# Attention stage of a fused kernel: the second chunk's projections laid over other units, later chunks turned two units later

## The chip, the cores and the metric

One core of one Trainium2 chip runs the whole program in one launch. The metric is the device time of one execution in microseconds (us), lower is better. The kernel before was timed three times.

## The reference

The input is x[8, 256, 128] in float32 (2048 tokens of 128 numbers). Four parts follow one another, each on the layernorm of x and added back to x: four Mamba layers, a feed-forward block with 4-bit block quantisation of inputs, weights and hidden values, an attention block, and the same feed-forward block again. The change touches the attention block alone, which computes:

```
qkv = layernorm(x) @ w_qkv.T + b_qkv            # 16 heads of 8 numbers
att = (q k^T) / sqrt(8) + bias[h, i - j]        # HoPE bias per head
att = softmax(where(j <= i, att, -inf))         # 256 x 256 per head
x   = x + (att v) @ w_proj.T + b_proj
```

## The kernel before, in words

The tokens lie in 16 tiles of 128, and in four chunks (0 to 3) of four tiles, which is two batches. Attention works through 64 **units** u; a unit is two heads of one batch (`where`, L1663), so 16 units make a chunk. The loop of every engine runs over the same list, `ITERATIONS` = -3 to 69 (L1476), and asks `iteration(u)` (L1525) what is to be done. A unit below 0 belongs to the lead.

In iteration u the pieces are, in order: `s` (the scores of unit u+3, for the row maxima alone), `t0` and `t1` (the turned scores of unit u), for odd u `peak` (the maxima of two units turned) and `mix` (probabilities times v, two units at a time, three units late), for even u `turn` (that result turned back), and every eight units `ctx` and `proj` (the output projection, of which `ctx` comes at u = 12, 20, 28, ... and `proj` one unit later). A chunk's inputs are made in four more pieces: `x` turns the normed rows with four TensorE transposes (`turn_x`, L1689), `q` and `k` are one projection each (`project`, L1696), `v` is four matmuls (`project_v`, L1702). Chunk 0 is made before the loop. Chunk 1 is made in the lead, one piece each in units -3 (x), -2 (q), -1 (k) and 0 (v). Chunks 2 and 3 are made at u % 16 = 2 (x), 6 (q), 8 (k) and 9 (v), so chunk 2 in units 2, 6, 8, 9 and chunk 3 in units 18, 22, 24, 25 (`EARLY` is 2).

Each piece needs a PSUM bank, and `Banks` (L1479) counts the uses in the order in which `iteration` names them: `s` alternates between two double banks s0 and s1; `t0` and `t1` have one each; `peak`, `turn`, `proj` and `v` share one bank, here called bank v; `mix`, `x`, `q`, `k` and `ctx` share another, bank a. A piece on TensorE waits until the use before it of its bank has been read.

Who reads what. On TensorE `both_scores` (L1735) starts each iteration with the two mask matmuls of the `s` bank (`mask_scores`, L1710); the turned scores wait until the maxima of their pair were added into q (`banks.wait_read(t, "peak", u // 2)`) and until the exponentials of the unit before left banks t0 and t1. On VectorE iteration u does, in this order: `add_row` of a peak (L1851), `norm.vector_normalise` of a chunk if u % 16 is 2 (L1057), the maxima of `s` (L1843, L1844), the reading of `turn`, `proj` and `v` (`values`, L1835), and `norm.vector_moments` if u % 16 is 0 (L1038, L1042). ScalarE does `exps` (two exponentials, L1958), then `norm.scalar_rstd` if u % 16 is 1, then the copies of `mix`, `x`, `q`, `k` and `ctx`: `copy_mixed` (L1965), `copy_x` (L1944, it also waits for the v projection of the chunk before, which reads the same xT), `add_bias` (L1950), `copy_context` (L1971). GpSimd masks the probabilities (`causal`, L1915) and adds the output bias (L1920). SyncE waits for each `add_bias` and then issues four DMAs (L1685) that lay q or k of the chunk into the strips of `att_qk`; the scores of chunk 1 read them first in iteration 13 (`s` of unit 16), and `add_bias` of chunk 2 waits for those of chunk 1.

Of the kernel before, what the change touches and what calls it, by code (L numbers as in the profile page):

```python
# [1474 lines left out]
MAX_ROW = 2 * HD  # L1475
S_LEAD, PV_LAG, TURN_LAG, OUT_LAG = 3, 3, 4, 12  # L1476
EARLY = 2
ITERATIONS = range(-S_LEAD, UNITS + 6)


class Banks:


    def __init__(self, core):
        ring, acc = core.ring, core.acc
        self.space = {"s0": ring[:, 0:2 * BANK], "s1": ring[:, 2 * BANK:4 * BANK], "t0": acc[:, 0:BANK], "t1": acc[:, BANK:2 * BANK],
                      "v": acc[:, 2 * BANK:3 * BANK], "a": acc[:, 3 * BANK:4 * BANK]}
        self.s_full = {n: core.sem(f"att_bank_{n}_filled") for n in self.space}
        self.s_read = {n: core.sem(f"att_bank_{n}_read") for n in self.space}
        self.uses = {n: 0 for n in self.space}  # L1490
        self.at = {}
        self.use("t0", "x", 0), self.use("v", "v", 0)
        for kind, name in (("q0", "s1"), ("q1", "s0"), ("q2", "t0"), ("k2", "t1"), ("q3", "s1")):
            self.use(name, kind, 0)
        for u in ITERATIONS:
            for kind, n in iteration(u):
                name = {"s": f"s{n % 2}", "t0": "t0", "t1": "t1", "peak": "v", "turn": "v", "proj": "v", "v": "v",
                        "mix": "a", "x": "a", "q": "a", "k": "a", "ctx": "a"}[kind]
                self.use(name, kind, n)
# [28 lines left out]
def iteration(u):  # L1528


    per, at = 2 * GROUPS // CHUNKS, []

    def piece(kind, n, count):
        if 0 <= n < count:
            at.append((kind, n))

    piece("s", u + S_LEAD, UNITS)
    piece("t0", u, UNITS)
    piece("t1", u, UNITS)
    if u % 2:  # L1540
        piece("peak", (u + 1) // 2, GROUPS)
        piece("mix", (u - PV_LAG) // 2, GROUPS)
        if (u - OUT_LAG - 1) % 8 == 0:
            piece("proj", (u - OUT_LAG - 1) // 8, BATCH)
        if 0 <= u and u % per == 9:
            piece("v", u // per + EARLY, CHUNKS)
    else:
        piece("turn", (u - TURN_LAG) // 2, GROUPS)
        if (u - OUT_LAG) % 8 == 0:
            piece("ctx", (u - OUT_LAG) // 8, BATCH)  # L1550
        for kind, when in (("x", 2), ("q", 6), ("k", 8)):
            if 0 <= u and u % per == when:
                piece(kind, u // per + EARLY, CHUNKS)
    if -S_LEAD <= u <= 0:
        at.append(("xqkv"[u + S_LEAD], 1))
    return at


# [71 lines left out]
def attention_stage(core, tiles, x):  # L1630
    nc, ident = core.nc, core.ident
    qk, xT, banks, norm = tiles.qk, tiles.xT, tiles.banks, tiles.norm
    with ExitStack() as stage:
# [24 lines left out]
        def ready(u, lag):  # L1658

            c, r = divmod(u - 8 - OUT_LAG - 1 - lag, per)  # L1660
            return c if r == 0 and 0 <= c < CHUNKS - 1 else None
# [15 lines left out]
        with nc.Block(no_gpsimd_drain=True) as block:  # L1677
# [10 lines left out]
            def _(t):  # L1688
# [115 lines left out]
                t.wait_ge(s_maskb, 2)  # L1804
                for u in ITERATIONS:
                    work = iteration(u)
                    both_scores(u + S_LEAD, u)
                    for kind, n in work:
                        if kind == "peak":
                            turn_peaks(n)  # L1810
                        if kind == "mix":
                            mix(n)
                        if kind == "turn":
                            turn_mixed(n)
                        if kind == "ctx":
                            turn_context(n)
                        if kind == "proj":
                            project_out(n)
                        if kind == "x":
                            turn_x(n)  # L1820
                        if kind == "q":
                            project(0, n)
                        if kind == "k":
                            project(1, n)
                        if kind == "v":
                            project_v(n)

            @block.vector
            def _(v):
                def values(c):  # L1830
                    banks.wait_filled(v, "v", c)
                    dst = vals[:, chunk(c), :, 0:HD]
                    src = banks.bank("v", c).rearrange("p (t h d) -> p t h d", t=CH_TILES, d=HD)
                    bias = tiles.bv[:, :].rearrange("p (h d) -> p h d", d=HD).unsqueeze(1).broadcast_to([P, CH_TILES, HEADS, HD])
                    banks.read(nc.vector.tensor_tensor(dst, src, bias, ALU.add), "v", c)  # L1835
# [11 lines left out]
                def add_row(g):  # L1847
                    b, hg = g // HGROUPS, g % HGROUPS
                    banks.wait_filled(v, "peak", g)
                    q = qk[:, 0, b // CH_BATCH, hg, b % CH_BATCH, :]  # L1850
                    banks.read(nc.vector.tensor_tensor(q, q, banks.bank("peak", g)[:, 0:SEQ], ALU.add), "peak", g)  # L1851
# [22 lines left out]
                v.wait_ge(s_npk, 1)  # L1874
                for u in ITERATIONS:
                    work = iteration(u)
                    for kind, n in work:
                        if kind == "peak":
                            add_row(n)
                    if 0 <= u and u % per == 2 and u // per + EARLY < CHUNKS:  # L1880
                        norm.vector_normalise(v, u // per + EARLY)
                    for kind, n in work:
                        if kind == "s":
                            peaks(n)
                    for kind, n in work:
                        if kind == "turn":
                            normalise_heads(n)
                        if kind == "proj":
                            add_out(n)
                        if kind == "v":  # L1890
                            values(n)
                    if 0 <= u and u % per == 0 and u // per + EARLY < CHUNKS:
                        norm.vector_moments(v, u // per + EARLY)
                    if ready(u, 1) is not None:
                        banks.wait_read(v, "proj", 2 * ready(u, 1) + 1)
                        x.norm.vector_moments(v, ready(u, 1))
                    if ready(u, 3) is not None:
                        x.norm.vector_offset(v, ready(u, 3))
                    if ready(u, 5) is not None:
                        x.vector_scales(v, ready(u, 5))  # L1900
                    if ready(u, 7) is not None:
                        x.q.vector_exponent(v, ready(u, 7))
                    if ready(u, 9) is not None:
                        x.q.vector_round(v, ready(u, 9))
# [34 lines left out]
            def _(a):  # L1939
# [32 lines left out]

                for u in ITERATIONS:
                    if 0 <= u < UNITS:
# [132 lines left out]
```

## Time and profile before

| what | us |
|---|---|
| median of three runs | 1041.48 (1040.91 to 1042.05) |
| the profiled execution's own time | 1041.14 |
| its span, first to last instruction | 1039.4 |
| TensorE busy in the span | 950.2 (91%) |
| VectorE, ScalarE, GpSimd busy | 902.7, 761.0, 760.1 |
| mean granted TensorE clock | 0.969 of full speed |

The time is 1.74 us longer than the span: that lies before the first and after the last instruction. The attention stage is the stretch from about 811 to 970 us of the span. Times in rows are us from the span's start unless marked ns; a matmul row's duration includes its drain, so neighbours overlap a little, and starts are a better ruler than durations. A granted clock of 1.00 is 2.4 GHz and 0.50 is 1.2 GHz.

### The profile page before, as it was taken

The numbers are of one execution on the slowest core, as the hardware profiler recorded it, in microseconds if no ns is written. First come the engines' busy times: TensorE is split into PE (matmuls) and PEld (weight loads), VectorE is DVE, ScalarE is ACT, GpSimd is POOL, SyncE is SP. The second block draws the span as 40 slices with busy tenths as digits, with TensorE's granted clock in tenths as the row PEclk, the third lists the DMA queues.
The fourth block names the chain that finished last, engine by engine and source line by source line (L and its number), as shares of the span: only waits on it lengthen the run. The fifth ranks groups of instructions, "written<-read, shape, count | busy, mean of one in ns | idle before, by whom it ended". The sixth has DMA issues, their size and how long they took to land. (4 is left out here: it accounts for less than half of the span.)

```text
span 1039.4 us, 29750 instructions
## 1 busy us (share of the span) xinstructions
PE 950.2 (91%) x11909; PEld 577.4 (56%) x11909; DVE 902.7 (87%) x1724; ACT 761.0 (73%) x1683; POOL 760.1 (73%) x426
## 2 busy tenths in 40 slices
PE   5799999999999999999999999987477899999775
PEld 2455555555555555555555565655256566666445
DVE  6889998999989999899998999998799657787597
ACT  5888898898988989889898898885333245555442
POOL 1688999989999999899998999997353323333243
PEclk9799999999999999999999999999798889999899
DMA  6845443544444444545445454430760110000001
GB/s 191 279 128 166 153 156 125 166 145 182 147 149 152 148 151 145 183 145 160 143 133 169 140 166 143 141 129 2 161 141 1 21 22 12 13 2 2 2 0 41
DMA packets 69272, 120.88 MB, mean 116 GB/s; under 512 B 40072, under 2 KB 51152, under 8 KB 60112
## 3 DMA queue, kind: packets, MB, share of 16 engines
q1 hardware_dynamic: 69136, 118.98, 36.3%
q8 instruction: 95, 1.56, 0.6%
q14 instruction: 41, 0.34, 0.1%
HBM read 111.10 MB, written 6.29 MB: 113 GB/s over the span
## 5 line engine op out<-in xcount | busy, mean ns | idle before, releaser
L902 DVE TENSOR_TENSOR_SCAN hid<-decay,acc 128x256 f32<-128x256 f32 x1024 | 604.6, 664 | 40.9 <-PE acc L539 40.5
L1002 POOL TENSOR_TENSOR prod<-hid,c_rep 128x1024 f32<-128x1024 f32 x256 | 600.1, 2373 | 44.3 <-DVE hid L902 33.3
L765 ACT ACTIVATE decay<-delta,a_neg 128x255 f32<-128x255 f32 x1024 | 428.2, 501 | 47.7 <-DVE hid L902 47.5
L539 PE MATMUL acc<-b_diag,du_t 64*64 64x256 f32 x4096 | 273.2, 383 | 15.9 <-DVE hid L902 12.2
L567 PE MATMUL ring<-prod,ident 64*64 64x256 f32 x4096 | 255.5, 379 | 2.2 <-POOL prod L1002 2.2
L539 PEld LDWEIGHTS acc<-b_diag,du_t 64*64 64x64 f32 x4096 | 147.8, 134 | 124.8 <-DVE hid L902 55.4
L567 PEld LDWEIGHTS ring<-prod,ident 64*64 64x64 f32 x4096 | 152.0, 133 | 83.5 <-issue 22.9
L1915 POOL TENSOR_SCALAR_AFFINE_SELECT att_probs<-att_probs 128x512 f32<-128x512 f32 x64 | 40.9, 639 | 109.3 <-ACT att_probs L1958 106.9
L1958 ACT ACTIVATE att_probs<-acc 128x384 f32<-128x384 f32 x128 | 55.8, 488 | 55.8 <-PE acc L1732 55.8
L444 PE MATMUL ring<-xpad,diag_cw 64*64 64x512 f32 x512 | 60.6, 590 | 0.0
L1116 POOL TENSOR_TENSOR ffn_h_value<-ffn_h,ffn_h_inv 128x704 f32<-128x704 f32 x16 | 23.7, 1479 | 43.5 <-DVE ffn_h_value L1139 32.5
L1130 ACT ACTIVATE ffn_h_step<-ffn_h_step,minus_step 128x704 f32<-128x704 f32 x16 | 14.1, 882 | 56.3 <-DVE ffn_h_step L1124 56.3
L1730 PE MATMUL acc<-att_qk 17*128 17x256 f32 x256 | 54.4, 440 | 0.5 <-ACT att_probs L1958 0.4
L1722 PE MATMUL ring<-att_qk 17*128 17x256 f32 x256 | 48.5, 440 | 0.6 <-DVE att_qk L1851 0.6
L1370 PE MATMUL ring<-wgT,ffn_xqT 128*128 128x352 f32 x64 | 30.1, 556 | 15.7 <-ACT ffn_silu L1430 9.5
L1843 DVE TENSOR_REDUCE att_npk<-ring 128x2 f32<-128x256 f32 x64 | 27.1, 423 | 19.7 <-PE ring L1721 19.5
L1844 DVE TENSOR_REDUCE att_npk<-ring 128x2 f32<-128x512 f32 x64 | 43.7, 683 | 0.0
L989 POOL TENSOR_TENSOR du<-delta,u 128x512 f32<-128x512 f32 x30 | 37.7, 1282 | 0.0
L1732 PE MATMUL acc<-att_qk 17*128 17x128 f32 x256 | 33.4, 276 | 0.0
L1732 PEld LDWEIGHTS acc<-att_qk 17*128 17x128 f32 x256 | 32.3, 192 | 0.7
L444 PEld LDWEIGHTS ring<-xpad,diag_cw 64*64 64x64 f32 x512 | 19.8, 134 | 22.7 <-issue 19.1
L427 PE MATMUL ring<-cur,wxi 128*128 128x512 f32 x60 | 31.5, 650 | 0.8 <-ACT cur L659 0.8
(180 smaller groups left out, 1259.5 us busy)
## 6 DMA issues: line engine op xcount, KB each, us to landing
c_rep<-c_rows SPq DMA_DIRECT2D x64, 1024.0 KB, 4.8
b_diag<-diag_rows SPq DMA_DIRECT2D x62, 512.0 KB, 3.8
diag_rows<-zeros SPq DMA_DIRECT2D x2, 2048.0 KB, 12.4
att_qk<-in_pos_q SPq DMA_DIRECT2D x4, 768.0 KB
att_qk<-in_pos_k SPq DMA_DIRECT2D x4, 768.0 KB
att_qk<-att_dense SPq DMA_DIRECT2D x24, 64.0 KB
resid<-in_x SPq DMA_DIRECT2D x4, 256.0 KB, 3.2
c_rows<-bc SPq DMA_DIRECT2D x64, 8.0 KB, 1.5
```

Source lines behind the costliest of these rows:

```text
L444: last = nc.tensor.matmul(out[h * HALF:(h + 1) * HALF, :], diag_cw[rows, lay(n) % 2, h, k, :], xpad[rows, h, :, k:k + SEQ], start=(k == 0) ...
L539: last = nc.tensor.matmul(inj[m * HALF:(m + 1) * HALF, K % 2, at:at + HALF * SG], du_t[rows, n % 2, e, chans:chans + HALF], b_diag[rows, K ...
L567: last = nc.tensor.matmul(y[h * HALF:(h + 1) * HALF, at], ident[rows, rows], prod[rows, H % PRODS, h, s, :], start=False, stop=(H % HSUMS ...
L765: last = nc.scalar.activation(decay[:, K % DECAYS, s, 1:], delta[:, n % 2, h, e * SEQ + 1:(e + 1) * SEQ], ACT.Exp, scale=a_neg[:, lay(n) % ...
L902: last = nc.vector.tensor_tensor_scan(hid[:, K % HIDS, s, :], decay[:, K % DECAYS, s, :], rows[:, s, :], 0.0, ALU.mult, ALU.add)
L1002: nc.gpsimd.tensor_tensor(prod[:, K // 2 % PRODS, h], hid[:, K % HIDS, :, :], c_rep[:, g, :, at], ALU.mult).then_inc(s_prod, 1)
L1722: return nc.tensor.matmul(out[:, P:SPAN], q[:, P:], k, start=False, stop=True, skip_group_check=True)
L1730: nc.tensor.matmul(out[:, 0:SEQ], k[:, 0:P], q, start=True, stop=True)
L1732: banks.fill(nc.tensor.matmul(out[:, SEQ:SPAN], k[:, P:], q[:, P:], start=True, stop=True), f"t{i}", u)
L1844: last = nc.vector.tensor_reduce(npk[:, g % 2, 1, at], score_bank(u)[:, :, P:SPAN], AX, ALU.max, negate=True)
L1915: nc.gpsimd.affine_select(at, at, [[0, 4], [1, P]], ALU.is_ge, zero, base=0, channel_multiplier=-1).then_inc(s_causal, 1)
L1958: banks.read(nc.scalar.activation(probs[:, g % 3, js[i], 0:SPAN], banks.bank(f"t{i}", u)[:, 0:SPAN], ACT.Exp, scale=SCALE), f"t{i}", u)
```

## The change

The pieces of chunk 1 are named by a small table, x in unit -3 (as before), q in -1, k in 1 and v in 2. The x piece of chunks 2 and 3 moves from u % 16 = 2 to u % 16 = 4, so from units 2 and 18 to units 4 and 20. Every engine, and the count of bank uses, takes its order from the same function.

```diff
 EARLY = 2
+FIRST_DENSE = {-3: "x", -1: "q", 1: "k", 2: "v"}
 ITERATIONS = range(-S_LEAD, UNITS + 6)
...
         if (u - OUT_LAG) % 8 == 0:
             piece("ctx", (u - OUT_LAG) // 8, BATCH)
-        for kind, when in (("x", 2), ("q", 6), ("k", 8)):
+        for kind, when in (("x", 4), ("q", 6), ("k", 8)):
             if 0 <= u and u % per == when:
                 piece(kind, u // per + EARLY, CHUNKS)
-    if -S_LEAD <= u <= 0:
-        at.append(("xqkv"[u + S_LEAD], 1))
+    if u in FIRST_DENSE:
+        at.append((FIRST_DENSE[u], 1))
     return at
```

## Rows read from the trace of the kernel before

**Rows 1.** Windows: from:to, length, PE, PEld, DVE, ACT, POOL busy (x), PEclk, DMA, GB/s.

```profile
880.00:920.00 40.00, 40.00 (x520) 27.18 (x517) 30.02 (x82) 22.59 (x56) 13.01 (x20) 1.00 0.07 13
```

**Rows 2.** Windows, the stretch of low clock after the lead.

```profile
826.23:839.88 13.65, 13.65 (x102) 7.11 (x104) 5.43 (x14) 4.78 (x11) 3.77 (x5) 0.50 0.01 1
```

**Rows 3.** Windows, units -3 to 7, each from its first mask matmul to the next unit's.

```profile
811.64:813.30 1.66, 1.66 (x17) 1.27 (x15) 1.43 (x3) 0.00 (x0) 0.00 (x0) 1.00 0.00 0
813.30:815.42 2.12, 2.12 (x14) 1.17 (x12) 1.57 (x4) 0.60 (x1) 0.00 (x0) 1.00 0.00 0
815.42:817.72 2.30, 2.30 (x15) 1.35 (x14) 0.84 (x3) 0.69 (x1) 0.00 (x0) 1.00 0.00 0
817.72:819.89 2.17, 2.17 (x27) 1.81 (x26) 1.54 (x4) 1.56 (x3) 0.00 (x0) 1.00 0.35 90
819.89:821.35 1.46, 1.46 (x23) 1.09 (x21) 1.44 (x6) 0.17 (x1) 0.64 (x1) 1.00 0.57 66
821.35:824.85 3.50, 1.78 (x24) 1.30 (x22) 3.47 (x15) 2.04 (x6) 1.18 (x2) 1.00 0.54 61
824.85:827.90 3.05, 3.05 (x38) 1.47 (x36) 1.62 (x4) 1.47 (x3) 0.85 (x3) 0.73 0.09 11
827.90:830.51 2.61, 2.61 (x24) 1.77 (x21) 0.39 (x2) 0.76 (x2) 1.10 (x1) 0.50 0.00 0
830.51:834.69 4.18, 4.18 (x37) 2.11 (x36) 2.33 (x7) 1.37 (x4) 1.27 (x2) 0.50 0.00 0
834.69:839.01 4.32, 4.32 (x26) 2.32 (x23) 1.42 (x5) 1.25 (x3) 0.64 (x1) 0.50 0.02 4
839.01:841.71 2.70, 2.70 (x38) 1.53 (x36) 0.67 (x2) 1.56 (x3) 0.00 (x0) 0.84 0.06 24
```

**Rows 4.** Timeline of TensorE: start, us, line, tiles, in brackets idle before and releaser.

```profile
814.46 1.13 PE L1700 MATMUL acc<-att_xT,att_wqkv 128*128 128x512 f32 x2
...
822.34 0.48 PE L1722 MATMUL ring<-att_qk 17*128 17x256 f32 x1 [0.61 <-DVE att_qk L1851]
...
824.39 0.63 PE L1693 MATMUL acc<-ident,normed 128*128 128x128 f32 x4 [1.12 <-DVE normed L1057]
```

**Rows 5.** Timeline of VectorE in units 0 to 2, same columns.

```profile
820.10 0.69 DVE L1835 TENSOR_TENSOR att_v<-acc,att_bv 128x512 f32<-128x512 f32 x1
820.70 0.86 DVE L1038 BATCH_NORM_STATS2 stats<-resid 128x6 f32<-128x128 f32 x4
...
821.89 0.39 DVE L1851 TENSOR_TENSOR att_qk<-att_qk,acc 128x256 f32<-128x256 f32 x1
...
823.13 1.11 DVE L1057 TENSOR_SCALAR normed<-resid,meanvar,rstd 128x128 f32<-128x128 f32 x4
```

**Rows 6.** Windows of later units at full clock: 15, 16, 18, 19, 20, 21.

```profile
857.84:860.63 2.79, 2.79 (x38) 1.75 (x35) 1.89 (x6) 1.63 (x4) 0.79 (x2) 1.00 0.02 6
860.63:862.10 1.47, 1.47 (x25) 1.10 (x22) 0.83 (x3) 0.50 (x2) 0.48 (x1) 1.00 0.02 6
864.89:867.43 2.54, 2.09 (x28) 1.52 (x25) 2.54 (x8) 1.36 (x5) 0.66 (x2) 1.00 0.00 0
867.43:869.75 2.32, 2.32 (x39) 1.37 (x36) 1.32 (x5) 1.47 (x3) 0.45 (x1) 1.00 0.03 7
869.75:871.42 1.67, 1.67 (x26) 1.31 (x23) 1.03 (x3) 0.71 (x2) 1.65 (x2) 1.00 0.00 0
871.42:874.55 3.13, 3.13 (x43) 2.15 (x40) 2.23 (x7) 2.08 (x6) 1.49 (x3) 1.00 0.00 0
```

**Rows 7.** Timeline of ScalarE at unit 20, same columns.

```profile
871.10 0.87 ACT L1958 ACTIVATE att_probs<-acc 128x384 f32<-128x384 f32 x2 [0.83 <-PE acc L1732]
871.85 0.39 ACT L1971 ACTIVATE att_ctxT<-acc 128x256 f32<-128x256 f32 x1
```

**Rows 8.** Timeline of SyncE: the eight DMA issues of chunk 1's strips.

```profile
816.34 5.85 SPq L1685 DMA_DIRECT2D att_qk<-att_dense  x8
```

## The prediction

> **What bounds the kernel now.** I read three views in this order. First the windows: in the middle of the attention stage TensorE is busy for 40.00 of 40 us at full clock, and the next one, VectorE, for 30.02 [rows 1]. So this stage goes at TensorE's pace, and what shortens TensorE's order there shortens the kernel. The same view, unit by unit, shows where the pace is not kept: the eleven units -3 to 7 take 30.07 us [rows 3], while later a plain pair takes 2.79 + 1.47 us [rows 6]. Two things are wrong in that lead. Unit 2 takes 3.50 us and TensorE works for 1.78 of them [rows 3]. And from 826.23 to 839.88 the granted clock is 0.50, though TensorE is never idle in those 13.65 us [rows 2]; the fall comes right behind unit 2.
>
> Then the timeline of TensorE says what unit 2 waits for: 0.61 us for the row maxima added into q, and 1.12 us for the normed rows of chunk 2, which its x piece turns [rows 4]. The timeline of VectorE says why both are late: in unit 0 it first reads v (0.69 us) and then does the moments of chunk 2 before it comes to that addition, and the normalising follows at 823.13 and ends at 824.24, when TensorE's x starts [rows 5]. The change takes x of chunk 2 out of unit 2 and v of chunk 1 out of unit 0, which are just these two.
>
> **What a piece costs.** By differences of rows at full clock. The scores of a unit alone: 813.30 to 814.46, 1.17 us with its gap [rows 3, 4]. Peak: unit 1, 1.46 - 1.17 = 0.29 [rows 3]. x: unit -3, 1.66 - 1.17 = 0.49. k, and q of the same shape: unit -1, 2.30 - 1.17 - 0.29 = 0.84. v: unit 0, 2.17 - 1.17 = 1.00. Turn: unit 16, 1.47 - 1.17 = 0.30 [rows 6]. An odd unit with peak and mix takes 2.79 behind a plain even one and 2.32 behind one that had an x [rows 6]: the plain one waits 0.47 us, because the exponentials of the unit before still hold the t banks. So a piece in an even unit gets up to 0.47 us back in the odd unit behind it, and a bare even unit loses them.
>
> **The lead, unit by unit, if the clock stays at 1.00.**
> - Unit -3, unchanged: 1.66. Unit -2, q gone: 1.17. Unit -1, q in place of k, of the same shape: 2.30.
> - Unit 0, v gone: 1.17. Unit 1 has the bare unit before it and gets k: 1.17 + 0.47 + 0.29 + 0.84 = 2.77. Unit 2 gets v and loses x and both waits: 1.17 + 1.00 = 2.17.
> - Unit 3 with peak and mix behind a loaded unit: 2.32. Unit 4 gets x: 1.47 + 0.49 = 1.96. Unit 5: 2.32. Unit 6 with q(2): 1.47 + 0.84 = 2.31. Unit 7: 2.32.
>
> The sum is 22.47 us against 30.07, **7.60 us less**. Of this 5.65 us are the clock: units 3 to 7 take 3.05 + 2.61 + 4.18 + 4.32 + 2.70 = 16.86 us [rows 3], and 2.32 + 1.47 + 2.79 + 2.31 + 2.32 = 11.21 at full clock. The other 1.95 are the two waits, 1.73, and x's place. The Trainium skill, TensorE: Matmul & The Clock Gate, section HAM oscillation, prices a throttled stretch as its length times one minus the clock's share. By it 13.65 us would cost 6.8 and the whole forecast would come out 1.2 us lower; the rows say 5.65, since waits do not shrink with the clock, and I take the rows.
>
> **Are the covers there?** In the new order VectorE finishes the maxima of unit 3 near 819.0, the moments (1.25 us with gaps) near 820.2, adds the maxima by 820.6, and unit 2 now starts at 813.30 + 1.17 + 2.30 + 1.17 + 2.77 = 820.71: just in time, with 0.1 us to spare. The normalising ends near 822.6 and x needs it at 826.7. Reading v falls near 823.5 to 824.1, and the peak of unit 3, in the same bank, wants it near 824.1: nothing, or 0.2 us. If these are late, VectorE's slack is gone by up to 0.69 + 1.11 us of its own work; I put 0.2 in the range. ScalarE's work is the same in another order; the k bias comes behind the rstd of unit 1 and ends near 821.8, and bank a is wanted by mix near 824.4.
>
> The DMAs of SyncE: eight issues in 5.85 us [rows 8], so 0.73 each. Those of k start about 821.8 instead of 818.6 and end by 824.8. Their first readers are the q bias of chunk 2 in unit 6, now near 832, and the scores in unit 13, so 7 us are left where there were 17: they cost nothing. If one lands later than that, the q bias alone waits, and TensorE behind it at bank a.
>
> **Chunk 3.** x leaves unit 18, where TensorE idles 0.45 us for VectorE (2.54 us, of which 2.09 busy [rows 6]), and goes to unit 20, behind `ctx`. Both use bank a, so x waits until ScalarE has copied the context: that ends at 871.85 + 0.39 = 872.24 [rows 7], and TensorE would be ready at 871.42 [rows 6]. With some 0.05 us for the signal this is a **new wait of 0.87 us**. Before, units 18 to 21: 2.54 + 2.32 + 1.67 + 3.13 = 9.66. After: 1.47 + 2.79 + (1.67 + 0.87 + 0.49) + (3.13 - 0.27) = 10.15, where 0.27 is what `ctx` had left of the 0.47. A loss of 0.49 us. Behind x in line on TensorE stands unit 21's work, all of it counted. Bounds: if the wait is fully hidden the four units gain 0.38; if the context copy comes behind the next thing that ScalarE waits for, they lose about 1.5. The row of the copy is the nearest, and I take it. Chunk 2's x, in unit 4, has no `ctx` before it; the mix that held bank a must be read for `turn` anyway, so it is free.
>
> **Sum.** 7.60 - 0.49 = 7.11 us less. The profiled execution took 1041.14 us, span 1039.4 and 1.74 around it, so 1034.1; it lies 0.34 below the median of the runs, 1041.48, so the forecast is **1034.4 us**. Everything after unit 7 is as before but for units 18 to 21, TensorE stays the bound to the stage's end, and the feed-forward block behind starts that much earlier. Only its own clock falls may shift by a microsecond either way.
>
> **Rivals.**
> 1. The clock falls all the same. For it: in the rows the fall came without any idle stretch over 1.12 us [rows 4], and the new order has the thinnest units, -2 and 0, without any projection, and a new wait of 0.47 in unit 1 and 0.87 in unit 20. Against it: later plain pairs have the same 0.47 us wait and run at 1.00 [rows 6], and unit 18 idles 0.45 without a fall. If it falls for the same 13.65 us, only the waits remain: 1.95 - 0.49 = 1.5 us less, 1040.0, which is no change that can be told. A fall of half that length costs 2.8, so 1037.2. The Trainium skill, same page, section A second HAM failure mode, says that TensorE idling briefly between groups of matmuls can be enough to make the clock swing; by it unit 20 could do so, 1040.0 again. The trace agrees that short waits can (unit 2), and disagrees that they must (unit 18). Chance 0.13 for the long one, 0.10 for a short one.
> 2. Slower: the clock falls early, in the bare units -2 to 0, and stays low until q(2) in unit 6, the piece behind which it rose before. Low units cost 4.18 - 2.79 = 1.39 more for an odd one and 2.61 - 1.47 = 1.14 for an even one, 2.0 with a projection [rows 3, 6]. Eight low units, -1 to 6, with four projections among them (4 x 2.0 + 2 x 1.39 + 2 x 1.14), come to 13.1 us, and less the 7.11 that is 6.0 slower than before: 1047.5. It decides from about 17 us of low clock on, where 5.65/13.65 = 0.41 us for each us of it eat up the 7.11. Against it: q, k and v are still among these units. Chance 0.07.
> 3. The waits go, but come back as others in the lead: VectorE's 0.1 us of slack in unit 2 is not there, its moments are late again and the clock stays up or falls by chance. With 1 us of waits and full clock 1035.4; that is inside the first forecast's own range.
>
> That the change does nothing is no rival: all engines take their order from the one function.
>
> **How the numbers follow.** About 0.2%, 2.1 us, is what a measurement of this kernel can tell from no change. My forecast with its own range, 1032.8 to 1036.0, has 0.70; the short fall 0.10; the long one 0.13; early and slower 0.07. Faster by over 0.2%: 0.70 + 0.10 = 0.80; within 0.2%: the long fall, 0.13; slower: 0.07. The range reaches from 1032.6 to the lower edge of the long fall, 1039.6.
>
> **What would show it.** In the profile after: granted clock 1.00 from 811 to 960 us; the start of unit 8's mask matmuls at 834.1 instead of 841.7; no wait for VectorE before L1722 in unit 2 nor before L1693 in unit 4; and before L1693 in unit 20 a wait of about 0.9 us for ScalarE's context copy L1971. A low clock anywhere between 815 and 850 would make the size wrong; a unit 8 later than 841.7 would make the sign wrong.

## The result, and the profile after

The changed kernel takes 1035.22 us (median of 8 executions, 1033.15 to 1038.04) and the kernel before 1040.63 (8 executions, the three known ones among them, 1036.65 to 1042.05). The ratio is 0.9957, with a 95% interval of 0.9940 to 0.9974: faster, by 4.5 us by the ratio and 5.4 by the medians. The forecast was 7.1 us less and 1034.4 us. The profiled execution took 1035.28 us with a span of 1033.6.

First the windows of the changed kernel, unit -3 to 7, cut as in [rows 3] (from:to, length, busy us of PE, PEld, DVE, ACT, POOL, clock, DMA share, GB/s):

```profile
811.61:813.26 1.65, 1.65 (x16) 1.27 (x14) 1.42 (x3) 0.00 (x0) 0.00 (x0) 1.00 0.00 0
813.26:814.43 1.17, 1.17 (x12) 0.78 (x10) 0.73 (x2) 0.60 (x1) 0.00 (x0) 1.00 0.00 0
814.43:816.82 2.39, 2.35 (x16) 1.36 (x15) 1.68 (x4) 0.00 (x0) 0.00 (x0) 1.00 0.00 0
816.82:818.00 1.18, 1.18 (x19) 0.82 (x18) 0.70 (x2) 0.69 (x1) 0.00 (x0) 1.00 0.00 0
818.00:821.01 3.01, 3.01 (x27) 1.97 (x24) 2.83 (x12) 2.06 (x6) 0.85 (x2) 1.00 0.20 59
821.01:823.18 2.17, 2.17 (x28) 1.81 (x26) 2.17 (x8) 1.64 (x4) 0.43 (x1) 1.00 0.37 46
823.18:825.49 2.31, 2.31 (x38) 1.36 (x35) 1.73 (x4) 0.87 (x2) 0.67 (x2) 1.00 0.25 68
825.49:827.39 1.90, 1.90 (x28) 1.54 (x25) 1.26 (x4) 0.99 (x3) 1.85 (x2) 1.00 0.20 53
827.39:829.71 2.32, 2.32 (x38) 1.36 (x36) 1.46 (x5) 1.68 (x4) 0.67 (x2) 1.00 0.01 2
829.71:832.03 2.32, 2.32 (x26) 1.40 (x23) 1.68 (x5) 1.26 (x3) 0.60 (x1) 1.00 0.04 7
832.03:834.35 2.32, 2.32 (x38) 1.37 (x36) 1.04 (x5) 1.56 (x3) 0.64 (x1) 1.00 0.03 11
```

TensorE's rows fill every one of them but for 0.04 us, the clock is 1.00 in all, and the eleven units take 22.74 us where they took 30.07 [rows 3]. Unit 8 starts at 834.35; the forecast said 834.1.

The timeline of VectorE in units 0 to 2, after (start, us, then what; compare [rows 5]):

```profile
819.09 0.86 DVE L1038 BATCH_NORM_STATS2 stats<-resid 128x6 f32<-128x128 f32 x4
...
820.35 0.42 DVE L1852 TENSOR_TENSOR att_qk<-att_qk,acc 128x256 f32<-128x256 f32 x1
...
821.62 1.11 DVE L1057 TENSOR_SCALAR normed<-resid,meanvar,rstd 128x128 f32<-128x128 f32 x4
```

The maxima of unit 2's pair are added by 820.77, 0.24 us before unit 2 begins at 821.01, and the normed rows are there at 822.73 for an x that comes at 826.96.

Units 18 to 21 of the changed kernel, windows and then the one wait in the timeline of TensorE:

```profile
857.53:859.00 1.47, 1.47 (x25) 1.10 (x22) 1.47 (x5) 0.61 (x3) 0.48 (x1) 1.00 0.00 0
859.00:861.96 2.96, 2.87 (x39) 1.76 (x36) 2.40 (x8) 1.63 (x4) 0.96 (x2) 1.00 0.02 6
861.96:865.00 3.04, 2.33 (x30) 1.73 (x27) 2.05 (x6) 1.53 (x4) 2.19 (x3) 1.00 0.00 0
865.00:867.86 2.86, 2.86 (x42) 1.90 (x40) 1.21 (x3) 1.86 (x4) 0.52 (x1) 1.00 0.00 0
```

```profile
864.51 0.66 PE L1694 MATMUL acc<-ident,normed 128*128 128x128 f32 x4 [0.71 <-ACT att_ctxT L1972]
```

The new wait is where it was expected, behind the copy of the context on ScalarE. Counted by starts it is 0.88 us (x begins at 864.51, and the unit's other pieces, 1.67 us, would end at 863.63) where 0.87 was forecast. The four units take 10.33 us against 9.66 [rows 6], a loss of 0.67 where 0.49 was forecast.

From unit -3 to unit 60 the changed kernel takes 141.25 us (811.61 to 952.86) and the kernel before 147.90 (811.64 to 959.54): 6.65 less in the attention stage. From unit 60 to the end it takes 80.64 instead of 79.86, at a mean clock of 0.85 instead of 0.91. The windows of that last stretch, before and after:

```profile
959.54:1039.40 79.86, 56.41 (x340) 40.10 (x336) 59.85 (x115) 31.64 (x67) 30.68 (x25) 0.91 0.05 14
```

```profile
952.86:1033.50 80.64, 60.48 (x340) 43.82 (x336) 59.85 (x115) 31.84 (x67) 30.70 (x25) 0.85 0.05 14
```

Nothing in it was changed; VectorE's work is the same 59.85 us. Over all the profiles here that stretch took between 79.9 and 83.3 us, and the start of unit -3 lay between 809.6 and 812.9. Both move the time of an execution by some microseconds whatever the lead does, so below the lead is measured by its own units and the time beside it.

### The profile page after: what moved, and what is told of

Read it like the earlier page. It is cut to its first block and busy times, and to the rows that moved or that the text cites. A ratio compares the mean times of both kernels' runs of the same rounds, so it can differ in the third digit from the quotient of the medians.

```text
span 1033.6 us, 29750 instructions
## 1 busy us (share of the span) xinstructions
PE 949.8 (92%) x11909; PEld 580.2 (56%) x11909; DVE 902.6 (87%) x1724; ACT 761.5 (74%) x1683; POOL 760.9 (74%) x426
```

## The experiments

The theory (A): TensorE's waits in the lead bring the clock down, and the change cures the fall by removing them. The rival (B): the fall comes from something else, such as the narrow score matmuls, or from where the projections stand.

**The new lead alone**, as an edit of the changed kernel.

```diff
-        for kind, when in (("x", 4), ("q", 6), ("k", 8)):
+        for kind, when in (("x", 2), ("q", 6), ("k", 8)):
```

> The new lead (q, k, v of chunk 1 in units -1, 1, 2), but x of chunks 2 and 3 stays in units 2 and 18. Theory A (the gain is a clock fall cured, and the fall comes from TensorE's waits being dense in units 1 and 2): x in unit 2 waits about 0.5 us for the normed rows that are ready at 822.6, nothing else waits; the clock stays at 1.00 from 811 to 960 us, unit 8 starts near 835.3, chunk 3 loses nothing; about 6.5 us less than before. Theory B (any wait before x in unit 2 brings the fall): low clock from 826 for about 13.65 us, unit 8 near 841, gain under 1.5 us.

Measured: 1037.11 us (10 executions), ratio 0.9960 (0.9939 to 0.9981). Timeline of TensorE, the wait before x in unit 2, and the window of units -3 to 7:

```profile
824.20 0.63 PE L1694 MATMUL acc<-ident,normed 128*128 128x128 f32 x4 [0.62 <-DVE normed L1057]
```

```profile
812.94:836.71 23.77, 23.11 (x261) 15.31 (x258) 16.79 (x45) 11.38 (x25) 5.68 (x8) 1.00 0.13 25
```

The clock stays at 1.00 with the 0.62 us wait in unit 2, and the eleven units take 23.77 us, 1.03 more than in the changed kernel. So this wait before x did not bring the fall here, and the spread lead does most of the work without the later x. The 6.5 us less of the expectation were counted against the longest fall of the kernel before (see below); by the ratio it is 4.2. The median is 1.9 us above the changed kernel's, but the two were timed apart and their ratios (0.9960 and 0.9957) do not differ. The units say 0.36 more: 1.03 in the lead, less the 0.67 that chunk 3 doesn't lose.

**The later x alone**, an edit of the kernel before, profiled twice.

```diff
-        for kind, when in (("x", 2), ("q", 6), ("k", 8)):
+        for kind, when in (("x", 4), ("q", 6), ("k", 8)):
```

> The old lead (x, q, k, v of chunk 1 in units -3 to 0), but x of chunks 2 and 3 in units 4 and 20. The 1.12 us wait before x in unit 2 is gone, the 0.61 us wait for the row maxima stays. Theory A: clock 1.00 through the lead, unit 8 near 834.9, so the moved x alone brings nearly all of the gain, 6.8 us in the lead and 6.1 after the loss at unit 20. Theory B (the spread projections are what keeps the clock up): the clock falls near 826 as before and unit 8 starts near 840.

Measured: ratio 1.0007 (0.9978 to 1.0035), and ten executions in two groups: five from 1035.81 to 1038.02 and five from 1043.26 to 1045.02. The profile is of the upper group (1044.84). Its waits in the timeline of TensorE, and its windows from unit 2 to unit 8 and of the low clock:

```profile
823.54 0.48 PE L1722 MATMUL ring<-att_qk 17*128 17x256 f32 x1 [0.61 <-DVE att_qk L1851]
...
826.52 0.49 PE L1758 MATMUL acc<-ident,att_npk 128*128 128x128 f32 x2 [0.17 <-DVE att_npk L1844]
```

```profile
822.54:842.67 20.13, 19.25 (x175) 11.24 (x172) 9.90 (x31) 8.46 (x20) 5.04 (x7) 0.66 0.11 15
826.71:840.37 13.66, 13.66 (x101) 7.57 (x100) 5.43 (x14) 4.34 (x10) 3.77 (x5) 0.50 0.00 1
```

> The same kernel as e2_x_only, looked at once more. Its times fell into two groups, 1035.8 to 1038.0 and 1043.3 to 1045.0, and its profile (1044.84) had the clock at 0.50 from 826.71 to 840.37. Theory A (the two groups are executions with and without the fall behind unit 2, which TensorE's waits of 0.61, 0.47 and 0.17 us bring about in some of them): a profile of the lower group shows the clock at 1.00 there and unit 8 some 6 us earlier after its unit -3; one of the upper group shows the fall again. Rival (the groups differ elsewhere, such as in the feed-forward stage): a lower profile shows the fall too.

This execution took 1036.86 us, which is the lower group. Its waits, and the same stretch, unit 2 to unit 8:

```profile
821.79 0.48 PE L1722 MATMUL ring<-att_qk 17*128 17x256 f32 x1 [0.61 <-DVE att_qk L1851]
...
824.77 0.41 PE L1758 MATMUL acc<-ident,att_npk 128*128 128x128 f32 x2 [0.17 <-DVE att_npk L1844]
```

```profile
820.80:834.74 13.94, 13.07 (x175) 8.33 (x172) 9.89 (x31) 8.39 (x20) 5.04 (x7) 1.00 0.17 21
```

This is the cleanest pair: one kernel, the same instructions, the same two waits, once with the fall and once without. The fall costs 20.13 - 13.94 = 6.19 us for 13.66 us of low clock. The two executions lie 7.98 us apart; of the rest, 1.75 us come before the lead, whose unit -3 starts at 812.84 in the one and at 811.09 in the other. The pair also shows that the fall is not a fixed property of a kernel: it comes in some executions. Theory A had expected none here. It was wrong in one of the two profiles and, if the groups of times are read as with and without the fall, in half of the ten executions.

**Work in the place of a wait.** In the kernel before, where TensorE waits for the normed rows:

```diff
                     banks.wait_free(t, "x", c)
+                    if c == EARLY:
+                        nc.tensor.matmul(banks.bank("x", c), tiles.wqkv[:, 1, :], xT[:, :], start=True, stop=True)
+                        nc.tensor.matmul(banks.bank("x", c)[:, 0:P], tiles.wqkv[:, 1, :], xT[:, 0:P], start=True, stop=True)
                     t.wait_ge(norm.s_norm, c + 1)
```

> The kernel before, with two surplus matmuls (512 and 128 columns, about 1.1 us together, their result overwritten at once) that TensorE does in unit 2 in the place of its 1.12 us wait for the normed rows. Nothing else is moved and no wait is shorter. Theory A (idle TensorE brings the clock down): the clock stays at 1.00, unit 8 starts near 836.1 instead of 841.7, 5.6 us less than before though work was added. Rival (the clock falls for a reason that has nothing to do with the idle time, such as the narrow score matmuls of units 1 to 5): it falls as before and the time is that of before, or 0.1 us more.

Measured: 1036.16 us (4 executions, 1035.56 to 1037.83), ratio 0.9960 (0.9945 to 0.9976). Units -3 to 7 at clock 1.00:

```profile
809.81:834.14 24.33, 23.72 (x264) 15.56 (x262) 16.70 (x45) 11.46 (x25) 5.69 (x8) 1.00 0.16 24
```

Surplus work made the kernel faster. The 24.33 us are 5.74 under [rows 3]; the 0.61 us wait is still there, unit 2 takes 3.48 us as against 3.50, and no piece moved, so nearly all of it is clock. [rows 3] has the longest of three falls: against the mean of the three profiles of the kernel before (30.07, and 28.49 and 25.88 below) it is 3.8 us, and the ratio says 4.2. The surplus work was tried in no other place, so it is not shown that it must lie in the wait. The same in the kernel with the later x, in the place of its 0.61 us wait:

```diff
+                    if u == 2:
+                        banks.wait_free(t, "mix", 0)
+                        nc.tensor.matmul(banks.bank("mix", 0)[:, 0:SPAN], tiles.wqkv[:, 1, :], xT[:, 0:SPAN], start=True, stop=True)
                     if turned:
                         banks.wait_read(t, "peak", u // 2)
```

> e2_x_only with one surplus matmul of 384 columns (about 0.63 us), done by TensorE in unit 2 in the place of its 0.61 us wait for the row maxima. Theory A (idle time brings the fall): the upper group vanishes, all times near 1035.5 to 1038. Rival (the narrow units alone bring it): two groups as in e2_x_only.

Measured: ten executions, nine from 1035.36 to 1038.55 and one at 1045.00, median 1036.2, ratio 0.9974 (0.9948 to 1.0000). The upper group is one of ten instead of five of ten. It did not vanish, as theory A had expected, and with ten executions each the difference can be chance (about one time in seven). Unit 2 to unit 8 takes the same time as in the lower group above, at clock 1.00:

```profile
821.11:835.04 13.93, 13.67 (x176) 8.62 (x173) 9.88 (x31) 8.39 (x20) 5.04 (x7) 1.00 0.17 21
```

**The kernel before, twice more.**

> The kernel before, looked at once more. Its 43 timed executions spread from 1035.5 to 1048.1. If the fall of the clock behind unit 2 is there in most executions but not in all, as in e2_x_only, a profile near 1036 to 1038 shows 1.00 and unit 2 to unit 8 in about 14.7 us, and one near 1040 or above shows the fall and 20.4 us. If it is there always, even a low one shows it.

> The same kernel and the same two expectations as e9_before_again.

The two took 1038.08 and 1042.21 us. Both have the waits of [rows 4] and both have the fall. The waits, the same in both:

```profile
823.46 0.48 PE L1722 MATMUL ring<-att_qk 17*128 17x256 f32 x1 [0.61 <-DVE att_qk L1851]
...
825.51 0.52 PE L1693 MATMUL acc<-ident,normed 128*128 128x128 f32 x3 [1.11 <-DVE normed L1057]
```

Windows of units -3 to 7 and of the low clock, the first and then the second:

```profile
812.76:838.64 25.88, 24.16 (x260) 15.41 (x258) 16.68 (x45) 11.47 (x25) 5.70 (x8) 0.93 0.15 22
826.63:830.05 3.42, 3.42 (x36) 1.54 (x28) 1.35 (x3) 1.31 (x4) 1.38 (x2) 0.50 0.00 0
```

```profile
811.68:840.17 28.49, 26.77 (x260) 16.52 (x258) 16.68 (x45) 11.47 (x25) 5.68 (x8) 0.82 0.14 20
826.16:836.40 10.24, 10.24 (x86) 5.49 (x90) 4.07 (x10) 3.38 (x8) 3.14 (x4) 0.50 0.01 2
```

So with the same program the fall lasts 13.65, 10.24 or 3.42 us, and the eleven units take 30.07, 28.49 or 25.88. Neither of the two expected pictures came (no fall, or the whole fall): what varies here is its length. In all four profiles with a fall it begins between 4.2 and 4.9 us behind the start of unit 2. What makes it longer or shorter, or leaves it out, these profiles do not show.

**Waits put back.** The changed kernel with x of chunk 3 in unit 18 (below), and surplus work on VectorE in unit 1, so that TensorE must wait though every piece keeps its new place:

```diff
+                    if u == 1:
+                        for i in (12, 13, 14, 15, 0, 1, 2, 3):
+                            nc.vector.bn_stats(core.stats[:, i, :], core.resid[:, i % 4 + 12, :])
```

> e4_x3_back with eight surplus statistics operations (0.22 us each) on VectorE in unit 1, ahead of the addition of the maxima, so that TensorE waits again: about 1.25 us in unit 2 and 0.6 in unit 3, 1.85 together, where the kernel before had 1.73. The pieces stay where the change put them. Theory A (waits of that density bring the fall): the clock falls behind unit 2 in most executions, unit 2 to unit 8 takes 20 to 21 us, the time is near 1040. Rival (the change's places, not its waits, keep the clock up): clock 1.00, unit 2 to unit 8 takes 15.2 us, time near 1034.3.

Measured: nine executions from 1035.39 to 1038.90, median of all ten 1037.32, ratio 0.9977 (0.9963 to 0.9991); a tenth took 1596.92 and is no part of the ratio. Waits in the timeline of TensorE, and unit 2 to unit 8:

```profile
822.20 0.48 PE L1725 MATMUL ring<-att_qk 17*128 17x256 f32 x1 [0.87 <-DVE att_qk L1854]
...
825.68 0.44 PE L1761 MATMUL acc<-ident,att_npk 128*128 128x128 f32 x2 [0.38 <-DVE att_v L1838]
```

```profile
820.95:835.68 14.73, 13.48 (x182) 8.84 (x180) 10.77 (x31) 7.98 (x18) 4.84 (x7) 1.00 0.17 28
```

No fall in this profile, with 1.25 us of waits; theory A expected one in most executions. The nine times hold none like 1043 to 1045, but a fall of 3.4 us costs some 1.5 us and could hide among them. The waits came out shorter than planned (1.25 for 1.85) and shorter than the 1.73 of the kernel before, so this does not refute that waits matter. They are longer than the 0.78 us of the later x alone, but part of a wait does not show as idle time between rows, because matmul rows overlap what follows. Starts are the better ruler. Units 1 to 3, first of this kernel and then of the later x alone in its profile without a fall:

```profile
817.94:820.95 3.01, 3.01 (x27) 1.97 (x24) 2.83 (x14) 2.06 (x6) 0.86 (x2) 1.00 0.20 59
820.95:824.06 3.11, 2.24 (x28) 1.80 (x26) 3.11 (x13) 1.63 (x4) 0.42 (x1) 1.00 0.34 62
824.06:826.82 2.76, 2.38 (x38) 1.36 (x36) 2.23 (x6) 0.87 (x2) 1.12 (x2) 1.00 0.46 58
```

```profile
819.35:820.80 1.45, 1.45 (x23) 1.08 (x20) 1.43 (x6) 0.17 (x1) 0.64 (x1) 1.00 0.58 66
820.80:822.82 2.02, 1.32 (x21) 0.85 (x19) 1.99 (x10) 1.23 (x5) 0.64 (x1) 1.00 0.53 59
822.82:825.88 3.06, 2.89 (x36) 1.81 (x37) 2.47 (x8) 1.69 (x4) 1.06 (x2) 1.00 0.37 43
```

Less the forecast's prices of their pieces (2.30, 2.17 and 2.32 here; 1.46, 1.17 and 2.32 there), units 2 and 3 lose 0.94 + 0.44 = 1.38 us here and 0.85 + 0.74 = 1.59 us in the later x alone, and unit 1 loses 0.71 here and nothing there. So which of the two waits longer depends on whether unit 1 is counted, and this run does not settle whether the length of the waits orders the kernels.

**Versions to beat it.** Chunk 3's x back in unit 18, chunk 2's still in unit 4:

```diff
+            if kind == "x" and u >= per:
+                when = 2
```

> The changed kernel with x of chunk 3 back in unit 18, x of chunk 2 still in unit 4. Expected: the wait of 0.71 us behind the context copy in unit 20 is gone and the 0.45 us wait in unit 18 is back; units 18 to 21 take 9.66 us instead of 10.33, so 0.67 us less than the changed kernel, 6.5 us less than before. Rival: the later position changes nothing, since the odd unit behind absorbs the difference: same time as the changed kernel.

Measured: 1032.44 us (4 executions), ratio 0.9928 (0.9911 to 0.9945). Units 18 to 21:

```profile
855.50:865.16 9.66, 9.22 (x127) 6.36 (x124) 7.12 (x20) 5.63 (x14) 4.25 (x6) 1.00 0.01 2
```

To that, chunk 3's moments, rstd and normalising in units 14, 15 and 16:

```diff
+NORMS = {0: 2, 14: 3}
...
-                    if 0 <= u and u % per == 2 and u // per + EARLY < CHUNKS:
-                        norm.vector_normalise(v, u // per + EARLY)
+                    if u - 2 in NORMS:
+                        norm.vector_normalise(v, NORMS[u - 2])
...
```

(The moments and the rstd are changed in the same way.)

> e4_x3_back with chunk 3's moments, rstd and normalising in units 14, 15 and 16 instead of 16, 17 and 18, x of chunk 3 still in unit 18. The 0.45 us wait before x in unit 18 should go: units 18 to 21 take 9.05 us instead of 9.65, so 0.6 us less than e4_x3_back. Rival: VectorE, now busier in unit 16, delays the maxima and the wait comes back one or two units earlier; no gain.

Measured: 1035.29 us (6 executions), ratio 0.9944 (0.9922 to 0.9965). The same units:

```profile
857.91:866.97 9.06, 9.06 (x126) 6.44 (x123) 5.98 (x16) 5.40 (x13) 4.09 (x6) 1.00 0.01 2
```

The wait is gone and the 0.60 us are there, but the time as a whole isn't lower: in its profile the stretch behind unit 60 took 83.3 us, in that of the version before it 80.0. And instead of the early norm, q of chunk 1 in unit 0:

```diff
-FIRST_DENSE = {-3: "x", -1: "q", 1: "k", 2: "v"}
+FIRST_DENSE = {-3: "x", 0: "q", 1: "k", 2: "v"}
```

> e4_x3_back with q of chunk 1 in unit 0 instead of -1, so that units -2 and -1 have no projection. The forecast's slower rival said that bare units can bring the clock down. If so: low clock within units -1 to 4 and 5 us or more lost. If waits and not bare units are the cause: clock 1.00, and the same time as e4_x3_back within 0.5 us, since q's 0.84 us are only moved and unit 1 gains the 0.47 us wait back.

Measured: 1035.01 us (5 executions), ratio 0.9938 (0.9917 to 0.9959). Units -3 to 7, with two units bare of projections:

```profile
811.69:834.20 22.51, 22.17 (x260) 14.54 (x257) 16.71 (x45) 11.26 (x25) 5.69 (x8) 1.00 0.17 26
```

The clock stays up through units -2 and -1; these bare units did not bring it down. Last, both together:

> e7_early_norm and e8_bare_lead together: q, k, v of chunk 1 in units 0, 1, 2, x of chunk 3 in unit 18 with its norm two units earlier. Unit -3 to unit 60 took 140.58 us in e4_x3_back, 140.16 in e7 and 140.37 in e8; together 139.95 is expected, 0.6 us under e4 and 1.3 under the changed kernel, and a time of 1034 give or take the microsecond or two by which the feed-forward stages differ between executions. Rival: the two overlap in no unit but VectorE becomes late somewhere; no better than e4.

Measured: 1034.55 us (6 executions, 1034.26 to 1034.89), ratio 0.9949 (0.9934 to 0.9964). From unit -3 (809.92) to unit 60 (949.84) it takes 139.92 us, as expected and the shortest of all, 1.33 under the changed kernel. The profile gives that back behind unit 60, at a mean clock of 0.79:

```profile
949.84:1033.10 83.26, 62.38 (x340) 44.43 (x336) 59.82 (x115) 31.75 (x67) 30.71 (x25) 0.79 0.05 13
```

By the intervals only the version with chunk 3's x back in unit 18 looks better than the changed kernel, and the two intervals overlap a little (0.9911 to 0.9945, and 0.9940 to 0.9974); its four executions are few. The units say that it saves 0.67 us, the times cannot confirm more.

## Why the forecast was right, and where it was off

**The two waits and their cause.** Right. The change takes both away: VectorE's moments still come before the addition of the maxima, but with v gone they no longer make it late, and the 0.1 us of slack forecast for unit 2 was 0.24. (x started at 824.39 before, not at 824.24 where the normalising ended; nothing hangs on it.)

**The lead, unit by unit.** Right within 0.27 us: 22.47 forecast, 22.74 measured. Unit 1 took 3.01 instead of 2.77: the wait behind a bare unit is 0.71 there and not the 0.47 of later pairs. The 0.47 was read behind an even unit that has its `turn` of 0.30 us; unit 0 has none, so it covers less of the exponentials. Unit -1 took 2.39 instead of 2.30.

**Chunk 3.** Right in place and cause, 0.67 for 0.49. Units 20 and 21 took 3.04 and 2.86, forecast 3.03 and 2.86. The missing 0.17 is in unit 19, 2.96 for 2.79. There VectorE does the normalising at 858.35 and reads the turned result (L1864) only from 860.54 to 860.77; the peak, which needs the same bank, starts at 860.82. With x gone from unit 18 TensorE gets there earlier and waits for it.

**The sum.** This step was mis-sized: the 5.65 us for the clock. The forecast took the 13.65 us fall of one profile as what the kernel before always does. It is the longest of three; the others are 10.24 and 3.42 us, and the lead took 30.07, 28.49 and 25.88 us. Against these the changed lead gains 7.33, 5.75 and 3.14, in the mean 5.4; less 0.67 for chunk 3 that is 4.7 us, and the ratio says 4.5. The single profile gains 1.9 us more than that mean, and the spread of the first three times (1.1 us) gave no hint of it: the eight executions spread over 5.4. That 1035.22 us still lie within 1032.8 to 1036.0 is partly luck: the 4.5 us of the ratio off the 1041.48 from which the forecast started would be 1037.0.

**The price per microsecond of low clock.** The forecast's 0.41 us for each (5.65 for 13.65) is borne out: 6.19 for 13.66 in the pair of one kernel is 0.45. With the lead at full clock taken as 30.07 - 5.65 = 24.42 us, the two shorter falls cost 4.07 for 10.24 and 1.46 for 3.42, 0.40 and 0.43. The Trainium skill, TensorE: Matmul & The Clock Gate, section HAM oscillation, gives one half; all four lie under it. The forecast's reason, that waits cost the same at either clock, fits but is not shown by itself: a plain odd unit, 2.79 us of which 0.47 were waiting, took 4.18 at the low clock, less than twice its 2.32 us of work.

**The rivals.** The first, that the clock falls all the same, did not come: the seven profiles of kernels with the new lead (the changed one and six of the variants) show 1.00 from unit -3 to unit 21. The second, slower through bare units, did not come either, nor did it with the two bare units side by side (-2 and -1). The third, new waits in the lead, came only as 0.24 us more than forecast in unit 1.

**The cause of the fall.** The forecast said: the idle time of TensorE in unit 2. For it: all three profiles of the kernel before have the two waits and the fall, and with work in the place of the longer one the clock stayed up (one profile at 1.00, four times of 1035.56 to 1037.83 where the kernel before had a median of 1040.94 beside them, and a ratio clear of 1). The other filled kernel adds one profile at 1.00, but so did the same kernel unfilled in one of its two. Against idle time as the whole cause: the later x alone, with the same waits in both profiles, fell in only one, and the kernel with waits put back was not seen to fall. What TensorE had to do around the waits may count as well: the later x alone has no projection in units 1 to 3, while the kernel with waits put back has k in unit 1 and v in unit 2. That would make the spread projections a second part of the cure, beside the waits, and the surplus matmuls would work by being more work, wherever they stand. No run separates the two, and this stays open.

## What to carry to other kernels

Where TensorE's pace sets the time, read the granted clock behind every short wait: here the stretch behind 1.7 us of waits lost up to 5.7 us more, and both the change of places and surplus matmuls in the longer wait got it back. Before a clock fall is priced from one profile, take two or three; its length in one program varied from 3.4 to 13.7 us. And when a piece is moved to be off one wait, look at who holds its bank at the new place: x in unit 20 got a 0.71 us wait for the 0.45 it had left.

## What the runs showed that was not expected

The same program with the same waits was once at full clock through the lead and once at half for 13.66 us, and its times fell into two groups 8 us apart, of which the fall explains 6.2. And the stretch behind the attention stage, whose instructions nobody touched, took 79.9 us in some profiles and 83.3 in others, with a mean clock between 0.91 and 0.79: enough to hide a gain of 1.3 us in the stage before it.
